# Statistics of the second norm: per token in the attention, or per gathered block of an expert

## The reference, cut to what matters

```python
def _layernorm(x, axis=-1, eps=1e-05):
    m = jnp.mean(x, axis=axis, keepdims=True)
    v = jnp.var(x, axis=axis, keepdims=True)
    return (x - m) / jnp.sqrt(v + eps)

x = x + jnp.tanh(g_xattn[0]) * _L0_xattn_ref(_layernorm(x, axis=-1), ctx_1024, Wq, bq, Wk, bk, Wv, bv)
x = x + jnp.tanh(g_ffn[0]) * _L0_ffn_ref(_layernorm(x, axis=-1), router_w, gate_w, up_w, down_w)

# _L0_ffn_ref, E = 8 experts, I = 704:
routing_indices = jnp.argmax(router_logits, axis=-1)
for e in range(E):
    xe = where(mask, hidden_states, 0.0)              # the tokens of expert e
    ye = silu(xe @ gate_w[e].T) * (xe @ up_w[e].T) @ down_w[e].T
    out = out + where(mask, ye, 0.0)
```

## Time and profile before

| | us |
|---|---|
| median of 3 runs | 196.61 (196.61 to 197.22) |
| the profiled execution, its own time | 195.64 |
| its span, first to last instruction | 193.9 |
| TensorE matmul busy | 172.1 (89%) |
| TensorE weight load busy | 158.0 (81%) |
| GpSimd busy | 142.2 (73%) |
| ScalarE busy | 113.4 (58%) |
| VectorE busy | 106.1 (55%) |
| mean granted TensorE clock | 0.957 of 2.4 GHz |

### The profile page before, as it was taken

How to read it: one execution, slowest core, us unless ns; L and a number is a source line. 1 busy time by engine, 2 the same in 40 slices (tenths; PEclk the granted TensorE clock), 3 DMA queues, 4 the chain that set the end, 5 groups by cost and what they waited for, 6 DMA issues and landing times.

```text
span 193.9 us, 4261 instructions
## 1 busy us (share of the span) xinstructions
PE 172.1 (89%) x1313; PEld 158.0 (81%) x1313; DVE 106.1 (55%) x328; ACT 113.4 (58%) x263; POOL 142.2 (73%) x138
## 2 busy tenths in 40 slices
PE   6999799998635969998999999999599999999960
PEld 2757588987633759997999999999499999999950
DVE  1869178889995116644636644536056544634730
ACT  0577667856269229866839877747497806513600
POOL 4000779999166899999999999999999989955021
PEclk9999999999995599999999999999979999999996
DMA  6999912819810304987148418615830121011010
GB/s 184 348 310 373 367 64 67 258 59 265 305 57 0 108 20 137 349 332 220 54 131 297 142 48 284 219 52 204 284 101 11 29 57 54 8 55 58 3 33 29
DMA packets 11854, 28.98 MB, mean 149 GB/s; under 512 B 2072, under 2 KB 8681, under 8 KB 10790
## 3 DMA queue, kind: packets, MB, share of 16 engines
q1 hardware_dynamic: 6464, 20.20, 31.2%
q0 software_dynamic: 1920, 4.53, 7.1%
q10 hardware_dynamic: 3430, 3.74, 5.5%
HBM read 24.26 MB, written 4.52 MB: 148 GB/s over the span
## 4 chain that ended last, share of the span: by engine, by line
PE 47%; POOL 24%; issue 14%; DVE 7%; DMA 3%; POOLq 2%; ACT 0%; ACTq 0%; DVEq 0%
PE ps L1226 13%; POOL wgu L545 12%; PE ps L1259 11%; POOL xin L617 5%; PE ps L1091 4%; POOL out L626 3%; PE ps L1013 3%; DMA xin<-x_rows,table 3%; PE ps L1076 3%; PE ps L1113 3%; POOL wd L561 3%; PE ps L1064 2%; PE ps L1002 2%; PE ps L998 1%; POOLq L344 1%
## 5 line engine op out<-in xcount | busy, mean ns | idle before, releaser
L1226 PE MATMUL ps<-xhT,wgu 128*128 128x256 f32 (+2 forms) x528 | 67.7, 288 | 2.7 <-DVE xhT L1525 1.8
L1226 PEld LDWEIGHTS ps<-xhT,wgu 128*128 128x128 f32 x528 | 66.3, 188 | 3.4 <-issue 2.0
L545 POOL TENSOR_TENSOR wgu<-raw_gu,wgu 128x1408 fp32r<-128x1408 f32 (+1 forms) x22 | 52.4, 2400 | 0.2
L1259 PE MATMUL ps<-wd,hT 128*128 128x256 f32 (+1 forms) x340 | 43.8, 288 | 0.4 <-issue 0.3
L1259 PEld LDWEIGHTS ps<-wd,hT 128*128 128x128 f32 (+1 forms) x340 | 42.1, 186 | 0.9 <-issue 0.7
L1542 DVE TENSOR_TENSOR ps<-V_all,ps 128x336 f32<-128x336 f32 x40 | 20.5, 512 | 27.0 <-ACT V_all L905 13.2
L626 POOL DMA_INDIRECT out<-xin,table x20 | 19.6, 981 | 15.5 <-DVE xin L1564 11.6
L561 POOL TENSOR_TENSOR wd<-both,wd 128x512 fp32r<-128x512 f32 (+1 forms) x12 | 28.7, 2404 | 0.2
L617 POOL DMA_INDIRECT xin<-x_rows,table x20 | 19.6, 978 | 5.7 <-issue 4.3
L905 ACT ACTIVATE V_all<-ps 128x336 f32<-128x336 f32 x40 | 17.9, 446 | 9.4 <-PE ps L1226 7.7
L1564 DVE SCALAR_TENSOR_TENSOR xin<-ps,tg,xin 128x256 f32<-128x256 f32 (+1 forms) x20 | 9.0, 480 | 23.1 <-PE ps L1259 23.1
(11 more groups left out here) (161 smaller groups left out, 223.5 us busy)
## 6 DMA issues: line engine op xcount, KB each, us to landing
raw_gu<-in_Wgu SPq DMA_DIRECT2D x8, 1408.0 KB, 6.9
both<-in_Wd SPq DMA_DIRECT2D x8, 640.0 KB, 4.2
x_rows<-x ACTq DMA_DIRECT2D x8, 256.0 KB, 2.8
xin<-in_x SPq DMA_DIRECT2D x7, 256.0 KB, 8.5
both<-in_WdL SPq DMA_DIRECT2D x16, 64.0 KB, 5.0
both<-in_ctxT ACTq DMA_DIRECT2D x2, 480.0 KB, 7.2
xin<-x_rows,table POOLq DMA_INDIRECT x20, 5.0
out<-xin,table POOLq DMA_INDIRECT x20
```

The lines of the kernel that those rows point to most:

```text
L545: pool.tensor_tensor(lo[where], raw[where], hi[where].bitcast(F32), ALU.subtract)
L1226: last = pe.matmul(ps[:, bank, 0:n], weights(j, w_part, c, i, kind), xhT[:, j % 2, x_part, c, 0:n], start=(c == 0 and (w_part, x_part) == ...
L1259: last = pe.matmul(y_of(j, k), hT[:, h_part, some], wd[:, j % SPLIT, i, w_part, :], start=(s == 0 and n == 0 and (k % 2 == 0 or j == E - 1 ...
```

## The change

The 16 bn_stats and 16 bn_aggr in the attention, the first guess, GpSimd's Newton iteration with `r3`, the product `rsel`, its 16 matmuls and the three sums are gone. In their place VectorE takes the statistics of the gathered rows in each seat: bn_stats and bn_aggr per block, a guess, and Newton's iteration on 128x3 values (`newton_fused`, ten instructions, nine of them in three rounds and one for the bias). Expert 0's are taken before `turned_x(0)`, expert 1's in the middle of expert 0 (after the second chunk), those of expert j + 2 at the end of expert j, ahead of `finish(j)`. ScalarE's `gathered(j, k)` waits for `v_stat` j + 1. On GpSimd `low_gu(1, 1)` moves from behind the gathers of experts 0 and 1 to the place of the Newton iteration, ahead of the wait for the table. The idle matmuls go from 28, 52 and 34 to 54, 104 and 140. The same edits are made in the surplus path (experts with more than 336 tokens), in which only waits and counts change here.

```diff
@@ GpSimd
             pool.iota(iota_hi..., ...).then_inc(k_pool, 1)
-            pool.wait_ge(v_guess, 1)
-            link(newton(pool, link, mv2[:, :, 0], rs2[:, 0, :], rs2[:, 1, :], ALL))
-            link(pool.tensor_copy(r3[:, 0], rs2[:]))
-            link(pool.tensor_tensor(rem[:, 1], rs2[:], r3[:, 0], ALU.subtract))
-            link(pool.tensor_copy(r3[:, 1], rem[:, 1]))
-            link(pool.tensor_tensor(rem[:, 0], rem[:, 1], r3[:, 1], ALU.subtract))
-            pool.tensor_copy(r3[:, 2], rem[:, 0]).then_inc(p_r3, 1)
+            low_gu(1, 1)
             for par in range(2):
                 pool.wait_ge(d_row[par], 16 * (B // 2))
...
             for j in range(AHEAD):
                 gather_full(j)
                 gather_rest(j)
-            low_gu(1, 1)
             low_gu_chunk(SPLIT - 1, 0, 1)
             low_gu_chunk(SPLIT - 1, 1, 1)
@@ ScalarE, gathered(j, k)
+                act.wait_ge(v_stat, j + 1)
                 act.activation(xh[0:BLOCK[k], k, :], seat(j, k), ACT.Identity,
                                scale=moment(j, k, 0), bias=moment(j, k, 1))...
...
-            act.wait_ge(v_stat, 1)
@@ TensorE
-            spin(28)
+            spin(54)
             pe.wait_ge(v_sort, 1)
...
-            spin(52)
+            spin(104)
...
-            pe.wait_ge(v_rsel, 1)
-            for t in range(NTOK):
-                last = pe.matmul(ps[:, 3, 0:6 * NT], ohlo[:, t, :], rsel[:, :, :, t].rearrange("p a n -> p (a n)"),
-                                 start=(t == 0), stop=(t == NTOK - 1))
-            last.then_inc(t_stat, 1)
-
-            spin(34)
+
+            spin(140)
@@ VectorE, attention and routing
-                dve.wait_ge(v_x1, i + 1)
-                statistics(i, 0)
                 if i + 2 < B:
                     minima(i + 2)
-                statistics(i, 1)
-                moments2(i)
...
-            dve.wait_ge(v_x1, B)
-            for k in range(TB):
-                statistics(B - 1, k)
-            moments2(B - 1)
-            dve.wait_ge(v_aggr, B)
-            guess(dve, link, mv2[:, :, 1], ALL).then_inc(v_guess, 1)
...
-            dve.wait_ge(p_r3, 1)
-            dve.tensor_tensor(rsel[:], ohhi[:].unsqueeze(1).to_broadcast(dims), r3..., ALU.mult).then_inc(v_rsel, 1)
...
-            dve.wait_ge(t_stat, 1)
-            link(dve.tensor_copy(flat, ps[:, 3, 4 * NT:6 * NT]))
-            link(dve.tensor_tensor(flat, ps[:, 3, 2 * NT:4 * NT], flat, ALU.add))
-            dve.tensor_tensor(flat, ps[:, 3, 0:2 * NT], flat, ALU.add).then_inc(v_stat, 1)
@@ VectorE, new
+            def statistics(j, n_tokens):
+
+                if j >= 2:
+                    dve.wait_ge(a_xh, FULL * (j - 1))
+                    dve.wait_ge(a_xh3, j - 1)
+                for k in range(FULL):
+                    landed(j, k)
+                    link(dve.bn_stats(stx[:, k, :], seat(j, k)))
+                for k in range(FULL):
+                    ins = dve.bn_aggr(mvx[:, k, :], stx[:, k, :])
+                link(ins)
+
+                def measure_rest():
+                    landed(j, FULL)
+                    size = BLOCK[FULL]
+                    dve.bn_stats(stx[0:size, FULL, :], seat(j, FULL)).then_inc(v_rest, 1)
+                    dve.wait_ge(v_rest, 2 * j + 1)
+                    dve.bn_aggr(mvx[0:size, FULL, :], stx[0:size, FULL, :]).then_inc(v_rest, 1)
+
+                third(dve, "dve", n_tokens, measure_rest, lambda: dve.sem_inc(v_rest, 2))
+                dve.wait_ge(v_rest, 2 * j + 2)
+                some = slice(0, BL)
+                link(guess(dve, link, mvx[:, :, 1], some))
+                newton_fused(dve, link, mvx[:, :, 0], normal[:, 0, j % 2, :], normal[:, 1, j % 2, :], some).then_inc(v_stat, 1)
@@ VectorE, experts(j)
                     gated(CI * j + s)
                     if s:
                         low_h(CI * j + s - 1)
+                    if j == 0 and s == 1:
+                        statistics(1, n_next)
...
                 if j + 1 < E:
                     turned_x3(j + 1, n_next)
+                if 2 <= j + 2 < E and j + 2 < len(sizes):
+                    statistics(j + 2, sizes[j + 2])
                 finish(j, n_tokens)
@@ VectorE, ahead of the experts
-            sizes = [count(dve, 0), count(dve, 1)]
+            sizes = [count(dve, 0), count(dve, 1), count(dve, 2)]
+            statistics(0, sizes[0])
             turned_x(0)
```

More of the change, by code:

```diff
@@ L213, in flamingo_moe @@
         mean_w, at = part(V_all, at, P)
-        rsel, _ = part(V_all[:, 0:NTOK * 3 * NT].bitcast(BF16), 0, 6, NT, NTOK)
-        sg, _ = part(V_all, NTOK * 3 * NT, 2, G)
+        sg, _ = part(V_all, 0, 2, G)
         free_m = MT[:].rearrange("p c n -> p (c n)")
@@ L227, in flamingo_moe @@
         rk, at = part(free_q, 0, NTOK, E)
-        rem, at = part(free_q, at, 2, 2, NTOK)
         beyond, at = part(free_q, at, E, MORE)
@@ L1303, in run @@
                                          start=(t == 0), stop=(t == NTOK - 1))
-                    for t in range(NTOK):
-                        last = pe.matmul(ps[:, 3, 0:6 * NX], ohlo_x[:, t, :], rsel_x[:, :, :, t].rearrange("p a n -> p (a n)"),
-                                         start=(t == 0), stop=(t == NTOK - 1))
                     last.then_inc(t_more, 1)
-                    pe.wait_ge(v_where, 2)
+                    pe.wait_ge(v_where, 1)
                 turn_x(j, None)
@@ L1385, in residual @@
                 ins.then_inc(v_x1, 1)
-            def statistics(i, k):
-                dve.bn_stats(st2[:, TB * i + k, :], x1[:, i % 2, k, :]).then_inc(v_chain, 1)
-                chained[0] += 1
-            def moments2(i):
-                dve.wait_ge(v_chain, chained[0])
-                for k in range(TB):
-                    ins = dve.bn_aggr(mv2[:, TB * i + k, :], st2[:, TB * i + k, :])
-                ins.then_inc(v_aggr, 1)
             def router_part(i):
@@ L1425, in _ @@
             dve.memset(oh[:, NTOK, :], 0.0)
+            dve.memset(mvx[:], 1.0)
             measured(2, 3)
@@ L1642, in run @@
                     where()
+                statistics(j, None)
                 turned_x(j)
```

52 lines of the change are left out of this document (20 added, 32 removed).

## The result

The changed kernel takes 244.49 us (median of 4 runs, 243.93 to 245.09) against 196.92 beside it (196.61 to 198.27): 1.2413 times as long, 95% interval 1.2347 to 1.2478. The forecast was 221.0 with a range from 199 to 230, so it is slower, as forecast, and by twice as much. The profiled execution took 243.93 us with a span of 242.1 (before 193.9), so 48.2 us are to be explained; the mean granted clock fell from 0.957 to 0.895. The ratios in this document leave out executions in a slower state or over 1.5% above a kernel's fastest, above all one of gathers_early, 249.42 us at a granted clock of 0.653.

A forecast was written before the change was run, and what follows sets the result against it. It took GpSimd's low weights and a late gather, then TensorE, to bound the expert stage, with VectorE's routing ahead. Span 193.9 + 14.2 + 5.6 + 9.2 - 4.6 = 218.3, giving 221.0 us; range 199 to 230.

The forecast's parts named there:

- Attention and table: Up to the table: GpSimd's low weights block VectorE's two-input products, v_sort 57.4 instead of 51.2, table 6.8 us later.
- From the landing to the first expert: After expert 0's gathers land: three steps held by low_gu(2), 8.8 to 9.8 us after landing; first expert at 85.3.
- Expert 0: Within expert 0: statistics(1) delays ScalarE, so TensorE waits 4.1 us, plus 1.5 for the lowered clock: 5.6 us.
- Experts 1 to 7: Later experts: third-block landings 5.6, about 2 for expert 6, clock 1.5, taken as 9.2 us; 15.4 with full blocking.
- rival 3: Whole kernel: full blocking all along, 15.4 for 9.2, and low clock in the spins: 227 to 230 us; chance 0.15.
- The clock: TensorE behind long gaps: the lowered clock costs 1.5 us, added in expert 0 and again in experts 1 to 7.
- The spins: Idle matmuls ahead of the table: 104 of them end at 64.1 or 66, against 62.7 for v_lo.
- give back 4.6 us and hardly more: Expert stage: relieving GpSimd can at most recover TensorE's 4.6 us of gaps and slow clock; subtracted in the sum.
- Rival 2: Not slower: landing is no wait, TensorE's slack covers VectorE, 4.6 us given back: 194.6 to 196.6 us; chance 0.18.

The follow-up runs named there:

- gathers_early: Changed kernel with Newton in PSUM, low_gu(1) and spins back, expert 1's statistics before expert 0, third blocks' and expert 2's gathers issued earlier: 196.69 us, ratio 1.0011.
- spins_back: Changed kernel with the idle matmuls at 28, 52 and 34 again: 240.28 us.
- low_behind_landing: Changed kernel, low_gu(1) back behind the gathers, eight small PSUM steps before expert 0's Newton, GpSimd awaiting landings before low_gu(1): one of several at 240.7 to 244.4 us.
- newton_psum: Changed kernel with Newton's two running values in PSUM, 16 steps instead of 12: 220.60 us, ratio 1.1202.
- no_newton: Changed kernel without guess and Newton steps, scale and bias set to 1: 212.59 us, ratio 1.0766.
- after_gathers_early: Changed kernel with only GpSimd's gathers reordered, third blocks and expert 2's gather ahead of the low weights: 237.29 us, ratio 1.2014.
- two_input_first: Changed kernel with low_gu(1) back behind the gathers and each statistics' first small step given two SBUF inputs: one of several at 240.7 to 244.4 us.

## Why the prediction was wrong

- **Attention and table.** Right. Two chained products were held to the ends of the two long instructions, though L1425 (the old L1467) slipped in 0.04 us ahead and its two followers were hit. `v_sort` came at 56.9 (forecast 57.4), the table at 67.8 (67.0).
- **From the landing to the first expert.** The mechanism was right, the size not: "one is held to the end of the first 3.2, one to the end of the second, one by the 0.46. That makes 8.8 to 9.8 after the landing". It was 14.0 (73.48 to 87.50): one step over both long instructions, and one more, L407, over a gather and `low_d` behind it, 4.00, which the sum had not looked at, because its queue ended with `low_gu(2)`. The start at 91.34 instead of 85.3 is this, 4.2 to 5.2, and 1.6 of a later landing. The forecast took the rule that held in the attention, one GpSimd instruction for each step, to a place where gathers stand directly ahead of the run, and there a step is held over more boundaries than one. That error cost no time here: one by one, the steps would have been held up to the same end of the run. The held L407 is the error that cost time, and whether it is held hung on less than a microsecond: it got in ahead of `low_d` in spins_back and low_behind_landing.
- **Expert 0.** A gap of 3.68 us released by ScalarE (forecast 4.1), and the expert 7.6 us longer, forecast 5.6: the low clock after the spins' end had its part in the first 42 matmuls.
- **Experts 1 to 7.** This is the step that failed: 9.2 taken, less 4.6 given back, and 20.5 measured. The text chose "9.2, since landing and blocking fall partly into one wait and only the landing has rows behind it at every step". The landings were the smaller part: 2.45 and 1.50 us of waiting, against held steps of 3.21, 2.72, 3.75, 2.99 and 3.79 us in the statistics of experts 2 to 6, 16.5 us. They do fall partly into one wait, as the text said, for without the held steps the waits for landings grow from 3.95 to 8.5 us (newton_psum). But the 9.2 had a price for the landings only and none for the held steps, and these were the larger part. newton_psum, no_newton and after_gathers_early part the two: having Newton's steps held costs 24 us in the whole kernel, the landings 7 beside it and 11 without it. Even rival 3, which had full blocking, had 15.4 for it. (The terms of the 9.2, that is 5.6, 2 and 1.5, add up to 9.1.)
- **The clock.** It was priced twice at 1.5. Each of six gaps was followed by 3 to 6 us at 1.2 GHz. With the stretch from 91.3 to 95.9 that is about 28 us of matmuls, counted over windows of one microsecond, so some 14 lost, against 1.7 before. The gaps in experts 1 to 5 add up to 16.2 us. With half of their slow stretches, 10, less the 4.9 of before (gaps 3.2, clock 1.7), that makes 21, and 20.5 were measured.
- **The spins.** Forecast at 1.4 to 3.3 us on the path to the table (64.1 or 66 against 62.7): spins_back measured 3.0 there, of which 1.8 reached the first gather.
- **What was left aside.** `low_gu(1)` moved ahead was said to be able to "give back 4.6 us and hardly more". In the kernel before that is about right: it gives back the 5.5 us that it costs. In the changed one it gave nothing, as GpSimd waited there for ScalarE's split for 21.77 us.
- **Rival 2** (not slower) decided from a cost of `statistics(1)` under 4.0 us. It wasn't met, and yet the kernel that is not slower exists: the change with Newton in PSUM, `low_gu(1)` and the spins back, and early statistics of expert 1 and early gathers (1.0011, 0.9978 to 1.0044). Against the kernel before with early gathers it is 2.0% slower.

The sum of it: forecast span 218.3, measured 242.1; 6.1 at the front, 2.0 in expert 0, 15.9 in the rest.

## What to carry to other kernels

Before small VectorE steps are put beside GpSimd's long instructions, list for each its inputs and GpSimd's whole run up to its next pause, and price the group of steps up to the end of that run, with what stands behind the next gathers too. In this kernel, putting one of the operands in PSUM took the price away. A wait that was harmless in the middle of a stage can end it when its consumer moves ahead: look at which transfers the new consumer needs, and issue these first. And count the clock with the gaps: here half of 3 to 6 us behind each gap of the changed kernel's experts (2.4 to 4.3 us). Between 1.65 and 2.70 us it went both ways in these runs, so a gap's length alone doesn't tell. And when an edit is meant to hold the clock up, look at the granted clock at that place, and not only at the mean of the kernel.

## What the runs showed of the hardware

- A VectorE step that GpSimd blocks is let in at the end of one GpSimd instruction (2.64 to 3.23 us) where GpSimd had paused ahead of its run. Where the run stood directly behind indirect DMA instructions, it was let in only at the end of the second of two long ones (6.61 us) or of the fourth of four (11.59 to 13.46 us). Form and size made no difference, nor did issue under the gather or 1.30 us into the run. Behind gathers the pause was tried in one run, and it isn't separated there from the landing that was waited for, nor from the moment of issue (0.53 us into the run).
- A step can be held before the long instruction's recorded start: 0.55 us ahead (83.50 against 84.05) and 0.56 ahead (189.19 against 189.75), while the gather before it was still running. Steps issued earlier under the same gathers ran free.
- Writes of GpSimd alone hold up one-input steps from SBUF to SBUF (1.2 to 1.3 us instead of 0.16 to 0.18 under memsets of 1.3), and not those with two inputs (0.29).
- With an operand in PSUM, 16 steps that stood beside the gathers and long instructions took 0.16 to 0.17 us each.
- After gaps of 2.4 to 4.3 us in the experts of the changed kernel TensorE was granted 1.2 GHz for 3 to 6 us; after gaps of 0.4 to 0.9 us in gathers_early it kept 2.4 GHz. In between, gaps of 1.95 us in the kernel before (with 0.34 more behind two matmuls) and of 2.00 in two_input_first were followed by 1.2 GHz; gaps of 1.65 us in no_newton, 1.82 in newton_psum, 2.05 in after_gathers_early and 2.70 in two_input_first were not.
